# Selective scan: half of its input products moved from VectorE to ScalarE and TensorE, C rows by broadcast DMA

## What is computed

```python
xz, z, B_s, C_s, dt_in = split(layernorm(x) @ W_in.T)      # B_s, C_s: 16 states per token
u     = silu(causal_conv4(xz) + conv_b)                    # 256 channels
delta = softplus(dt_in @ W_dt.T + b_dt)
def step(h, inp):                                          # over 256 tokens
    dt_t, u_t, b_t, c_t = inp
    dA = exp(dt_t[..., None] * A)                          # A: 256 channels x 16 states
    h  = dA * h + dt_t[..., None] * b_t[:, None, :] * u_t[..., None]
    return h, einsum('bdn,bn->bd', h, c_t)
y = (scan(step) + u * D) * silu(z)
```

## Time and profile before

| | us |
|---|---|
| median of 3 runs | 810.67 (810.49 to 811.27) |
| the profiled execution, its own time | 813.47 |
| its span | 811.6 |
| busy: PE / DVE / ACT / POOL | 655.6 / 656.4 / 394.0 / 430.4 |
| scan stage, from TensorE's first row matmul to the last gate | 75.9 to 299.2 |

### The profile page before, as it was taken

The page is one execution under the profiler, slowest core; times in us unless marked ns, Lnnn a source line. Parts: engine busy times, 40 slices in busy tenths (PEclk is TensorE's granted clock), DMA queues, the critical chain, the costliest instruction groups (busy, mean ns, idle before and its releaser), DMA issues. The chain is left out here.

```text
span 811.6 us, 13798 instructions
## 1 busy us (share of the span) xinstructions
PE 655.6 (81%) x4594; PEld 413.9 (51%) x4608; DVE 656.4 (81%) x1551; ACT 394.0 (49%) x626; POOL 430.4 (53%) x380
## 2 busy tenths in 40 slices
PE   2994877778678771674889999999999999888985
PEld 1342333333333341562667666666667666756763
DVE  4478999999999969465788888888888888768976
ACT  1786555555555512554555444444444444255641
POOL 6113666666666646755455555555555555542222
PEclk9997899999999996697899999999999999899998
DMA  8000000000000000000000000000000000000000
GB/s 313 2 1 0 0 0 0 1 0 0 0 0 0 0 1 0 0 1 0 2 2 11 11 5 15 0 19 0 16 0 19 0 3 14 2 1 2 14 14 26
DMA packets 8151, 10.09 MB, mean 12 GB/s; under 512 B 1712, under 2 KB 6448, under 8 KB 7728
## 3 DMA queue, kind: packets, MB, share of 16 engines
q1 hardware_dynamic: 8112, 9.60, 3.6%
HBM read 8.55 MB, written 1.05 MB: 12 GB/s over the span
## 5 line engine op out<-in xcount | busy, mean ns | idle before, releaser
L540 POOL TENSOR_TENSOR arena<-arena 128x1024 f32<-128x1024 f32 x64 | 151.0, 2360 | 73.1 <-DVE arena L918 66.0
L918 DVE TENSOR_TENSOR_SCAN arena<-arena,psum 128x1024 f32<-128x1024 f32 x64 | 143.1, 2275 | 0.0
L675 ACT ACTIVATE arena<-arena 128x510 f32<-128x510 f32 x128 | 85.1, 712 | 100.5 <-DVE arena L918 97.6
L480 POOL TENSOR_TENSOR ve<-mv,eps 128x4 f32<-128x4 f32 x52 | 15.9, 305 | 209.9 <-DVE mv L832 209.9
L1231 PE MATMUL psum<-arena,Cs 128*128 128x512 f32 x256 | 121.1, 596 | 2.4 <-POOL arena L540 2.4
L1218 PE MATMUL psum<-arena,Sel 128*128 128x512 bf16 x178 | 51.4, 396 | 60.9 <-DVE arena L918 53.1
L587 POOL TENSOR_TENSOR arena<-arena,mhalf 128x32 f32<-128x32 f32 x16 | 86.8, 5427 | 3.1 <-DVE arena L1043 3.1
L913 DVE TENSOR_TENSOR psum<-arena,psum 128x1024 f32<-128x1024 f32 x64 | 75.1, 1218 | 2.7 <-PE psum L1218 2.7
L1218 PEld LDWEIGHTS psum<-arena,Sel 128*128 (+1 forms) x192 | 17.7, 99 | 112.8 <-issue 65.1
L1344 PE MATMUL psum<-arena,Wl 128*128 128x512 f32 x128 | 67.0, 635 | 8.4 <-DVE arena L1027 5.2
L1153 PE MATMUL psum<-Cs,arena 128*128 128x128 f32 x240 | 40.4, 295 | 40.1 <-ACT arena L689 23.3
(11 more groups left out here) (163 smaller groups left out, 1373.7 us busy)
## 6 DMA issues: line engine op xcount, KB each, us to landing
Wl<-wl SPq DMA_DIRECT2D x4, 384.0 KB, 3.1
Wa<-wa SPq DMA_DIRECT2D x1, 1251.0 KB, 7.2
Wd<-wd SPq DMA_DIRECT2D x1, 1100.0 KB, 12.7
X<-x SPq DMA_DIRECT2D x4, 256.0 KB, 7.8
Sel<-sel SPq DMA_DIRECT2D x1, 1024.0 KB, 10.5
Wl<-wl SPq DMA_DIRECT2D x4, 256.0 KB, 2.7
out<-X SPq DMA_DIRECT2D x4, 256.0 KB, 2.3
Cs<-const SPq DMA_DIRECT2D x1, 614.0 KB, 10.0
```

What stands on the lines that cost most here:

```text
L540: pool.tensor_tensor(Hc[:, h], Hs[:, r, h], Crows[:, r], ALU.mult).then_inc(hc_ready, 1)
L675: ins = act.activation(Da[:, h, group(e)].rearrange(seq, s=S)[:, :, 1:], Dt[:, h, group(g)].rearrange(seq, s=S)[:, :, 1:], ACT.Exp, scale= ...
L918: dve.tensor_tensor_scan(Hs[:, r, h], Da[:, h], pair_rows[h], 0.0, ALU.mult, ALU.add).then_inc(scanned, 1)
```

## The change

Rounds with an odd number are now "turned". In them neither the selector matmul for B nor VectorE's multiplication is used. The product is made token-major, where B is one value for each partition (token):

- Once for each group TensorE transposes `Dtu` (8 transposes of 128x128, a "flip") into a row buffer, and ScalarE copies the result, 128x1024, to `Flip[g % 2]`. The flip of group 0 comes after the first two fills, the others three rounds ahead of their group.
- B in token-major form (`Bt_rows`, 128x512) comes from 16 further matmuls ahead of the scan stage and one copy on ScalarE.
- For each turned round ScalarE makes 8 instructions of 128x256, in two parts of 4 (one part for each state): `Flip` times a column of `Bt_rows`, into `Wslot`. They stand behind the decays of the even round before.
- TensorE transposes these products back, 8 transposes for each half, into a row buffer, and VectorE's scan reads them there.

C rows come in another way in all rounds. ScalarE keeps an fp32 copy of the B and C rows in each of the four groups ahead of the scan (`Cf`, 32x512), SyncE writes the C part to a DRAM tensor, and in the scan stage SyncE fetches two rows for each round, each repeated on all 128 partitions (512 KB written), into `Crows[turn % 2]` once GpSimd is done with the round two before. C matmuls and copies on ScalarE are gone.

Banks 2 to 7 are now three row buffers of 128x1024, taken in turn by B rows, turned products and flips (`FILL_ORDER`). All loops of the stage are written out. On TensorE, between any two fills stands one `add_states`, and it is for the half-round four places behind the fill.

```diff
+TURNED = [t for t in range(ROUNDS) if t % 2 == 1]
+FLIP_AHEAD = 6
+def fill_order():
+    fills = []
+    for q in range(2 * ROUNDS):
+        turn, h = divmod(q, 2)
+        g, place = divmod(turn + FLIP_AHEAD // 2, STATE_PAIRS)
+        if h == 0 and place == 0 and 0 < g < G:
+            fills.append(("flip", g, 0))
+        fills.append(("turned" if turn in TURNED else "rows", turn, h))
+        if q == 1:
+            fills.append(("flip", 0, 0))
+    return fills
...
-        pair_rows = [psum[:, (4 + 2 * h) * GC:(6 + 2 * h) * GC] for h in range(HALVES)]
+        row_buffer = [psum[:, (2 + 2 * i) * GC:(4 + 2 * i) * GC] for i in range(3)]
...
# SyncE
+            for turn in range(ROUNDS):
+                g, pair = divmod(turn, STATE_PAIRS)
+                sync.wait_ge(hc_ready, turn * 2 + 2)
+                sync.dma_start(Crows[:, turn % 2].rearrange("p (e c) -> p e c", e=2),
+                               c_dram[2 * pair:2 * pair + 2, group(g)].unsqueeze(0).broadcast_to((P, 2, GC))).then_inc(c_in[turn % 2], 16)
# ScalarE, ahead of the scan
+                act.copy(Cf[0:32, group(g)], bank[g % 2][0:32, :]).then_inc(c_kept, 1)
...
+            act.copy(Bt_rows, bank[6]).then_inc(bt_ready, 1)
# ScalarE, scan stage
-                        act.wait_ge(c_rows, turn + 1)
-                        act.wait_ge(hc_ready, turn * 2 + 2)
-                        act.copy(Crows[:, r], psum[:, 2 * GC:4 * GC]).then_inc(c_copied, 1)
...
+            def keep_flip(g):
+                act.wait_ge(flipped, g + 1)
+                if g == 0:
+                    act.wait_ge(c_out, 16 * G)
+                act.copy(Flip[g % 2], row_buffer[FLIP_OF[g] % 3]).then_inc(flip_ready, 1)
+            def token_products(n, part):
+                g, pair = divmod(TURNED[n], STATE_PAIRS)
+                if n >= 2:
+                    act.wait_ge(b_rows, 2 * TURNED[n - 2] + 2)
...
+                for k in range(GT):
+                    column = (g * GT + k) * 2 * NSTATE + 2 * pair + part
+                    ins = act.activation(Wslot[n % 2][:, part, k, :], Flip[g % 2][:, k * 256:(k + 1) * 256], ACT.Identity,
+                                         scale=Bt_rows[:, column:column + 1])
+                ins.then_inc(w_ready, 1)
# VectorE
+                if turn not in TURNED:
+                    input_products(turn)
+                for h in range(HALVES):
...
+                    dve.wait_ge(da_ready, turn * 2 + h + 1)
+                    dve.wait_ge(hc_ready, turn * 2 + h + 1)
+                    dve.tensor_tensor_scan(Hs[:, turn % 2, h], Da[:, h], rows_of(turn, h), 0.0, ALU.mult, ALU.add).then_inc(scanned, 1)
+                    if g and place == 0:
                         gate_rows(g - 1, h)
# TensorE
+            for q in range(2 * ROUNDS + 2):
+                while filled < len(FILL_ORDER) and filled <= (FILL_OF[divmod(q + 2, 2)] if q + 2 < 2 * ROUNDS else len(FILL_ORDER)):
+                    fill(filled)
+                    filled += 1
+                if q >= 2:
+                    turn, h = divmod(q - 2, 2)
...
+                    add_states(turn, h)
```

More of the change, by code:

```diff
@@ new lines, in decays @@
+            def decays(turn, h):
+                g, pair = divmod(turn, STATE_PAIRS)
+                act.wait_ge(scanned, turn * 2 + h + 1)
+                seq = "p (b s) -> p b s"
+                for e in range(2):
+                    ins = act.activation(
+                        Da[:, h, group(e)].rearrange(seq, s=S)[:, :, 1:],
+                        Dt[:, h, group(g)].rearrange(seq, s=S)[:, :, 1:], ACT.Exp,
+                        scale=Aneg[:, 2 * pair + e + h * NSTATE:2 * pair + e + h * NSTATE + 1])
+                ins.then_inc(da_ready, 1)
@@ new lines, in _ @@
+            todo = [(n, part) for n in range(len(TURNED)) for part in range(2)]
+            for turn in range(ROUNDS):
+                g, place = divmod(turn, STATE_PAIRS)
+                for h in range(HALVES):
+                    decays(turn, h)
+                    if turn == 0 and h == 0:
+                        keep_flip(0)
+                    if place == STATE_PAIRS - FLIP_AHEAD // 2 and h == 1 and g + 1 < G:
+                        keep_flip(g + 1)
+                    while todo and TURNED[todo[0][0]] <= turn + (1 if todo[0][1] == 0 or h == 1 else 0):
+                        token_products(*todo.pop(0))
@@ L1214, in _, with fill @@
             pe.wait_ge(z_ready, 2 * G)
[L1215 to L1219, removed]
+            def fill(n):
+                what, turn, h = FILL_ORDER[n]
+                rows = row_buffer[n % 3]
+                if n >= 3:
+                    before, of, half = FILL_ORDER[n - 3]
+                    if before == "flip":
+                        pe.wait_ge(flip_ready, of + 1)
+                    else:
+                        pe.wait_ge(scanned, of * 2 + half + 3)
+                if what == "flip":
+                    pe.wait_ge(dtu_ready, 2 * turn + 2)
+                    for k in range(GT):
+                        for half in range(HALVES):
+                            ins = pe.transpose(rows[:, tile(k * HALVES + half)],
+                                               Dtu[:, half, turn * GC + k * P:turn * GC + (k + 1) * P], ident)
+                    ins.then_inc(flipped, 1)
+                    return
+                g, pair = divmod(turn, STATE_PAIRS)
+                if what == "turned":
+                    slot = TURNED.index(turn)
+                    pe.wait_ge(w_ready, 2 * slot + 2)
+                    for e in range(2):
+                        for k in range(GT):
+                            ins = pe.transpose(rows[:, tile(e * GT + k)], Wslot[slot % 2][:, e, k, tile(h)], ident)
+                else:
+                    for e in range(2):
+                        state = 2 * pair + e
+                        ins = pe.matmul(rows[:, group(e)], Sel[:, tile(state)], Bc[:, group(g)], start=True, stop=True)
+                ins.then_inc(b_rows, 1)
             def skip_row(g, h):
@@ L1232, in add_states @@
                 ins.then_inc(hc_used, 1)
[L1234 to L1242, removed]
             pe.wait_ge(bc_ready, G)
```

116 lines of the change are left out of this document (52 added, 64 removed).

## The result

| | before | after |
|---|---|---|
| median (lowest to highest), us | 810.97 (810.49 to 812.07) | 801.60 (799.19 to 803.85) |
| the profiled execution, its own time | 813.47 | 800.74 |
| its span | 811.6 | 798.6 |
| scan stage, first row matmul to last gate | 223.3 | 202.9 |
| everything behind the scan stage | 512.4 | 520.3 |

The ratio is 0.9882, interval 0.985 to 0.9914. The kernel became faster by 9.4 us, where 20.5 were forecast; the interval of the ratio doesn't reach 1. The time lies inside the range of the prediction, 11.6 us above its forecast. The two lower lines of the table say where the difference is: the scan stage gave 20.4 us, and the stages behind it, which the change doesn't touch, took 7.9 back. (The two profiled executions differ by 13.0 in span, 0.5 of it because the stage begins earlier; the medians of four runs each by 9.4.)

The account below looks back on a forecast made before the run. VectorE was taken to set the pace in the scan stage. The terms -35.8 + 7.0 + 1.2 + 2.7 + 3.8 + 0.6 = -20.5 us took 810.67 to 790.2 us, with a range from 783 to 802.

Parts of the forecast that it names:

- rival 1: Hand-over between ScalarE, TensorE and VectorE is late in each pair of rounds; 796 to 806 us, chance 0.15.
- What goes: Scan stage: VectorE no longer multiplies in 16 of 32 rounds, 35.8 us as ceiling; pairs of rounds take 10.98 us.
- Group changes: At 3 changes of group VectorE's gate waits 2.35 us for add_states behind a turned fill, 7.0 us in all.
- Flips: Groups 1 to 3: the flip holds a buffer, so the turned fill waits; 3 x 0.4 = 1.2 us.
- End: End of the scan stage: GpSimd lags, last gate ends 8.0 us after the last scan, 5.3 before; cost 2.7 us.
- Start: Scan start: flip 0 is on the path; delays 2.3, 1.4 and 1.5 us, less 1.4 held before, cost 3.8 us.
- Ahead of the scan: Before the scan stage: 4 more PSUM copies on ScalarE make the last group's chain come 0.6 us later.
- rival 3: TensorE's clock falls in the scan stage; 915 us at half clock, 802 for a tenth of the stage; chance 0.03.
- rival 2: Scan stage: C rows by DMA arrive late and GpSimd waits; 828 us at a landing of 8.5 us; chance 0.08.
- threshold of 6.1: Landing of C rows, in us, at which a pair of rounds reaches 10.98 us; beyond it, 16 x (landing - 6.1).

Follow-up runs that it names:

- a_shift97: The changed kernel with 97 do-nothing instructions on TensorE, so its layer loop begins at place 203 as in the kernel before: 790.86 us, ratio to before 0.9738.
- a_shift107: The changed kernel with 107 do-nothing instructions on TensorE, so its layer loop begins at place 213: 790.80 us, one execution.
- c_only: The changed kernel without turned rounds or flips, C rows by DMA, buffers and written-out loops kept, layer loop at place 203: 813.17 us, ratio to before 1.0021.

## Why the prediction was wrong

**The step that failed** is its last one: "Everything behind the scan stage is untouched." The code there is untouched and its time is not, because TensorE's code of the scan stage, now written out, puts the layer loop 927 instructions further back (3178 - 2251), from place 203 to 106. The two jumps back cost 9.9 us. It is a term that the sum lacked, and it reconciles the time: 790.86 with the place restored, 801.60 without. The prediction did name a change of the stages behind the scan as a sign of being wrong, but gave it neither a price nor a chance. The rivals had a time for this result (rival 1: 796 to 806), by a cause that didn't happen. Someone who had compared only the times would have settled on it.

**The scan stage came out nearly as forecast.** Of the forecast 20.5, the terms inside the stage are 21.1 (the sum without the 0.6 ahead of it), and the stage gave 20.4. Part of that closeness is luck, since errors cancel:
- *What goes.* 32 multiplications, pairs at 10.97 us: right.
- *The hand-over, rival 1.* ScalarE's products last 493 ns (predicted 500), four in a row 1.69 us (1.64). No wait in the middle of a group but those behind flips and behind the dips of the clock, below.

```profile
L745 ACT ACTIVATE arena<-arena 128x256 f32<-128x256 f32 x128 | 54.1, 493 | 0.0
```

- *Group changes.* Three waits of 2.13 us are 6.4; predicted 7.0.
- *Flips.* Three waits of 0.42 us (one is at 114.63 above) are 1.3; predicted 1.2.
- *End.* The last scan ends at 270.28 and the last gate at 278.29, 8.0 us, as predicted.
- *Start.* Waits of 1.97, 1.34 and 0.27 us behind the first multiplication (predicted 2.3, 1.4 and 1.5), 3.6 where 5.2 were counted; less the 1.4 that went it is 2.2 in place of 3.8. The oversized part is the 1.5 for skip rows and `add_states` at a low clock.
- *Ahead of the scan.* 0.6 us was counted for the copies of `Cf`. TensorE's first row matmul starts at 75.39, 0.5 earlier than before (75.88). But VectorE's first multiplication, at 76.16 in after, starts at 76.66 in a_shift97 and 77.94 in a_shift107, with the same code ahead of it, so one trace each can't tell a cost of 0.6.
- *TensorE's clock, rival 3.* The granted clock was 1.00 in most of the stage. Twice, at about 143.9 and 191.7 us, it fell for 3.4 us, to a mean of 0.83 in the ten us around. Behind that VectorE waits 0.34 + 0.89 and 0.89 us, 2.1 in all, for which the sum had no term. In a_shift107 neither the dips nor these waits are there, while the three of 0.42 remain. This is rival 3 on a small scale. What brings the dips is open; c_only, in which no product is transposed, has three of them from 115 to 150 us (0.85 in the mean). Between the two dips of after, from 150 to 190 us, TensorE is busy for 36.4 of 40 us with as many transposes, at 1.00, so the transposes as such didn't take the clock away.

The terms as measured are -35.8 + 6.4 + 1.3 + 2.1 + 2.7 + 2.2 = -21.1, against -20.4 of the stage; 0.7 is left unexplained.

- *C rows, rival 2.* The landing was sized too small:

```profile
arena<-c_rows_by_state SPq DMA_DIRECT2D x32, 512.0 KB, 4.8
```

4.8 us where 3.5 were taken from plain loads, half of the way to the threshold of 6.1. GpSimd never waited for it, so it cost nothing.

The Trainium skill, page "TensorE: Matmul & The Clock Gate", Part 4: PE-mode transpose, had given about 275 ns for a transpose and a clock gate that transposes don't engage. The trace agrees with the 275 ns as the length of one transpose's record (shortest, median, longest in ns):

```profile
L1326 PE MATMUL psum<-Cs,arena x256: 272/273/447, 84.3 to 266.4; 128*128 128x128 f32 x128
```

But the records overlap: a turned fill of eight takes 1.04 to 1.09 us at a granted 1.00, 0.13 each, so 275 ns is not the price of one in a row, and the rows that the prediction took instead held. No run here shows transposes without other matmuls around them, so what they do to the clock by themselves is open.

## What to carry to other kernels

A stage that isn't edited can still change its time through the place of its code. Where a change makes an engine's program longer ahead of a long hardware loop (here 1783 instructions), look at the packets of the instruction queue, at the length of the jump instruction and at waits "issue" behind it, and try the loop at another place with instructions that do nothing before you explain the time by the edited stage. Inside the edited stage the sum by rows of the timeline held to 1 us, and its largest waits (gates behind a turned fill) named the reordering that gave another 11 us.

## What was not expected of the hardware

- Program code is fetched in packets of 16 KB, about 256 instructions. With TensorE's loop of 1783 instructions at a good place, no packet is fetched in its later turns; at a bad one packets are fetched in every turn, TensorE waits 3.3 to 4.1 us at each jump back (6.3 and 6.7 at place 193), and a jump back costs 4.6 to 8.9 us in all. The jump instruction lasts 0.21 to 0.24 us at a good place and 3.3 to 4.2 at a bad one.
- Part of that is the clock: behind the two gaps in TensorE's work (3.30 and 3.9 us) the granted clock was 0.50 (1.2 GHz), from 498.9 to 502.3 us and from 587.6 to 591.0 in after, and four matmuls took 3.50 us in place of 1.98.
- The rule that sets the good places (what is kept, and when it is thrown away) is open; runs at other places or with a loop of another length would tell.
- 512 KB spread by DMA from 4 KB of DRAM to 128 partitions land after 4.8 us, where a plain 384 KB takes 3.1.
